# A gated cross-attention and MoE kernel: weight units and first tile re-timed, and half of P's low parts moved to VectorE in the last batch

## What is computed

```
x = x + tanh(g_xattn) * (softmax(q k^T / 8) v) @ Wout      # q from LN(x), k and v from [LN(ctx), LN(x)]
s = softmax(LN(x) @ gate_w); top 2 of 8, renormalised
x = x + tanh(g_ffn) * sum_k s_k * (gelu(LN(x) @ w1[e_k] + b1[e_k]) @ w2[e_k] + b2[e_k])
```

## Time and profile before

| what | us |
|---|---|
| median of 3 runs | 1759.96 (1757.61 to 1762.75) |
| the profiled execution | 1763.63 |
| its span, first to last instruction | 1761.8 |
| TensorE busy | 1652.8 (94%) |
| VectorE, ScalarE, GpSimd busy | 1261.0, 1233.0, 1283.2 |

### The profile page before, as it was taken

The page is one execution under the profiler, slowest core; times in us unless marked ns, Lnnn a source line. Parts: engine busy times, 40 slices in busy tenths (PEclk is TensorE's granted clock), DMA queues, the critical chain, the costliest instruction groups (busy, mean ns, idle before and its releaser), DMA issues.

```text
span 1761.8 us, 42393 instructions
## 1 busy us (share of the span) xinstructions
PE 1652.8 (94%) x14916; PEld 1151.1 (65%) x14916; DVE 1261.0 (72%) x3018; ACT 1233.0 (70%) x2806; POOL 1283.2 (73%) x1448
## 2 busy tenths in 40 slices
PE   3999999999999999999999999999976988899997
PEld 1556666666666666666666666665655777788886
DVE  6777777777877777777777777788865765555553
ACT  3687888878777887877788878877766654444442
POOL 4477888787878888888989879987666554355444
PEclk9999999999999999999999999999988999999999
DMA  4368777777667778767776767755669865444443
GB/s 148 66 128 145 146 146 137 149 149 147 139 136 151 139 140 152 146 138 136 140 146 140 144 132 136 149 107 101 128 136 209 207 134 102 88 73 70 71 68 31
DMA packets 634297, 226.80 MB, mean 129 GB/s; under 512 B 573930, under 2 KB 624914, under 8 KB 633708
## 3 DMA queue, kind: packets, MB, share of 16 engines
q1 hardware_dynamic: 617964, 207.41, 58.6%
q0 software_dynamic: 15552, 16.67, 6.7%
q10 hardware_dynamic: 576, 0.01, 0.0%
HBM read 67.72 MB, written 16.83 MB: 48 GB/s over the span
## 4 chain that ended last, share of the span: by engine, by line
PE 78%; DVE 10%; ACT 4%; issue 3%; POOL 2%; DMA 2%; SPq 0%; POOLq 0%; ACTq 0%; DVEq 0%
PE proj_ps L1446 37%; PE scores_ps L1619 10%; PE scores_ps L1489 9%; PE proj_ps L1632 9%; PE tail_ps L1545 4%; PE pv_ps L1524 4%; PE pv_ps L1526 2%; DVE passed L1090 2%; ACT v_sb L884 2%; DVE v_sb L1245 2%; ACT p_space L804 1%; PE scores_ps L1446 1%; DVE k_lo L1239 1%; POOL p_parts L638 1%; PE proj_ps L1593 1%
## 5 line engine op out<-in xcount | busy, mean ns | idle before, releaser
L638 POOL TENSOR_TENSOR p_parts<-p_space,p_parts 112x487 f16<-112x487 f32 x512 | 560.7, 1118 | 106.4 <-ACT p_parts L813 104.0
L804 ACT ACTIVATE p_space<-scores_ps,shift 112x487 f32<-112x487 f32 x508 | 335.2, 664 | 7.9 <-POOL p_parts L638 5.2
L1090 DVE TENSOR_SCALAR_CACHE_REDUCE passed<-scores_ps 112x487 f16<-112x487 f32 x502 | 302.7, 661 | 24.0 <-PE scores_ps L1489 23.8
L870 ACT ACTIVATE k_hi<-proj_ps 128x488 fp32r<-128x488 f32 x250 | 144.5, 578 | 216.9 <-PE proj_ps L1446 215.3
L813 ACT ACTIVATE p_parts<-p_space 112x487 f16<-112x487 f32 x512 | 276.5, 607 | 0.0
L1245 DVE SCALAR_TENSOR_TENSOR v_sb<-proj_ps,v_sb 128x512 f16<-128x512 f32 x251 | 173.4, 691 | 139.4 <-ACT v_sb L884 128.7
L919 ACT ACTIVATE g_space<-scores_ps,b_sb,undo 128x256 f32<-128x256 f32 x280 | 139.2, 560 | 186.4 <-PE scores_ps L1619 180.9
L1524 PE MATMUL pv_ps<-v_sb,pt_space 128*128 128x128 f16 x2048 | 217.9, 221 | 13.4 <-DMA pt_space<-p_parts 12.0
L1239 DVE TENSOR_TENSOR k_lo<-proj_ps,k_hi 128x488 fp32r<-128x488 f32 x250 | 166.0, 664 | 81.2 <-ACT k_hi L870 79.0
L1619 PE MATMUL scores_ps<-xt_space,arena 128*128 128x256 f16 x1680 | 198.7, 280 | 18.6 <-DVE arena L1135 12.7
L1446 PE MATMUL proj_ps<-kv_hi,wkv_hi 128*128 128x488 f16 x500 | 186.7, 373 | 12.6 <-DVE v_sb L1245 9.3
(11 more groups left out here) (287 smaller groups left out, 3545.9 us busy)
## 6 DMA issues: line engine op xcount, KB each, us to landing
w_part<-in_L_ffn_w_dram SPq DMA_DIRECT2D x64, 256.0 KB, 3.8
arena<-in_L_ffn_w_dram SPq DMA_DIRECT2D x27, 512.0 KB
ctx_sb<-in_ctx_dram SPq DMA_DIRECT2D x32, 375.0 KB
pt_space<-p_parts SPq DMA_TRANSPOSE x256
x_sb<-in_x_dram SPq DMA_DIRECT2D x32, 112.0 KB
res_sb<-in_x_dram SPq DMA_DIRECT2D x32, 112.0 KB
out_dram<-x_sb SPq DMA_DIRECT2D x32, 112.0 KB
xn_dram<-xn SPq DMA_DIRECT2D x32, 112.0 KB
```

The lines of the kernel that those rows point to most:

```text
L638: pool.tensor_tensor(p_parts[0:LQ, p % PS, h, 1, 0:LK], p_f[0:LQ, p % 2, h, 0:LK], p_parts[0:LQ, p % PS, h, 0, 0:LK], ALU.subtract).then_i ...
L804: act.activation(p_f[0:LQ, p % 2, h, 0:LK], score_bank(p, h)[0:LQ, 0:LK], ACT.Exp, bias=shift[0:LQ, p // 2 % 2, n:n + 1], scale=-1.0, accu ...
L1090: dve.tensor_scalar(passed_of(p, h), score_bank(p, h)[0:LQ, 0:LK], P_SHIFT, None, ALU.add, ALU.min, accum_out=shift[0:LQ, p // 2 % 2, n:n ...
```

## The change

The units' tables are rewritten: units 1 to 7 are loaded and units 1 to 3 split earlier, units 15 to 31 are split earlier, and the last loads are spread. Units 1 to 3 get staging room of their own (`EARLY_SLOTS`, in expert 1's region, free once all projections are done). Both turns of rows are at step 251. TensorE makes the first two hidden chunks of tile 0 ahead of step 256. GpSimd writes one entry a step from step 258 on instead of two from step 256 on (two again in the last two steps). `xn16` lies elsewhere, so that unit 19 needs no wait for stores. In the last batch the low part of P for the second head of each pair is made by VectorE, behind the minima of an even step, with a semaphore of its own (`p_low1`) that SyncE and ScalarE wait for besides `p_low`.

```diff
-        if t >= PAIRS:
-            room = 2
+        if t >= PAIRS + 2:
+            room = 1 if t < LAST_STEP - 1 else 2
...
-SPLITS = {-7: (0,), -2: (1,), -1: (2,), 0: (3,), 1: (4,), 2: (5,), 3: (6,), 4: (7,), 7: (8,), 9: (9,), 10: (10,), 11: (11,), 13: (12,), 14: (13,), 15: (14,), 17: (15,),
-          18: (16,), 19: (17,), 21: (18,), 24: (19,), 25: (20,)}
+SPLITS = {-7: (0,), -5: (1,), -4: (2,), -3: (3,), 0: (4,), 1: (5,), 2: (6,), 4: (7,), 6: (8,), 7: (9,), 9: (10,), 10: (11,), 11: (12,), 13: (13,), 14: (14,), 15: (15,),
+          17: (16,), 18: (17,), 19: (18,), 21: (19,), 22: (20,), 23: (21,), 25: (22,)}
 SPLITS = {PAIRS + n: units for n, units in SPLITS.items()}
-TILE_SPLITS = {6: (21,), 7: (22, 23), 8: (24, 25), 9: (26, 27), 10: (28, 29), 11: (30, 31)}
-LOADS = {-16: (0,), -4: (1, 2), -3: (3,), -2: (4,), 0: (5,), 1: (6,), 2: (7,), 4: (8,), 5: (9, 10), 6: (11,), 9: (12,), 11: (13,), 12: (14,), 13: (15,),
-         14: (16,), 15: (17,), 16: (18,), 18: (19,), 19: (20,), 20: (21,), 22: (22,), 26: (23,)}
+TILE_SPLITS = {6: (23, 24), 7: (25, 26), 8: (27, 28), 9: (29, 30), 10: (31,)}
+LOADS = {-16: (0,), -8: (1,), -7: (2,), -6: (3,), -4: (4,), -3: (5,), -2: (6,), -1: (7,), 4: (8, 9), 5: (10, 11), 7: (12,), 8: (13,), 10: (14,), 11: (15,), 12: (16,),
+         14: (17,), 15: (18,), 16: (19,), 18: (20,), 19: (21,), 20: (22,), 22: (23,), 23: (24,), 24: (25,), 26: (26, 28)}
 LOADS = {PAIRS + n: units for n, units in LOADS.items()}
-TILE_LOADS = {6: (24, 28, 29), 7: (25,), 8: (26, 27), 11: (30, 31)}
+TILE_LOADS = {6: (27, 29), 8: (30,), 9: (31,)}
...
-FILL_STEPS = (PAIRS - 5, PAIRS - 3)
+FILL_STEPS = (PAIRS - 5, PAIRS - 5)
...
+        def wait_low(engine, p):
+
+            if p < LAST_PAIR:
+                engine.wait_ge(p_low, 2 * p + 2)
+            else:
+                engine.wait_ge(p_low, LAST_PAIR + p + 1)
+                engine.wait_ge(p_low1, p - LAST_PAIR + 1)
...
                 if u == 1:
+                    sp.wait_ge(proj_done, len(UNITS))
+                if u == 4:
                     sp.wait_ge(pv_done, PAIRS - NP)
...
             def p_low_of(p):
-                for h in range(2):
+                for h in range(2 if p < LAST_PAIR else 1):
...
-                if u == 8:
-                    act.wait_ge(unit_low, 8)
+                if u in (4, 8):
+                    act.wait_ge(unit_low, u)
...
+            def p_low_of(p):
+
+                dve.wait_ge(p_high, 2 * p + 2)
+                dve.tensor_tensor(p_parts[0:LQ, p % PS, 1, 1, 0:LK], p_f[0:LQ, p % 2, 1, 0:LK], p_parts[0:LQ, p % PS, 1, 0, 0:LK], ALU.subtract).then_inc(p_low1, 1)
+
             def unit_low_of(u):
 
-                if u == 19:
-                    for s in range(2):
-                        dve.wait_ge(stored[s], NB // 2 * 32)
...
+                if t % 2 == 0:
+                    for p in (t - 2, t - 1):
+                        if is_pair(p) and p >= LAST_PAIR:
+                            p_low_of(p)
...
             for i in range(-1, TILES):
-                for t in drain(i, 0):
-                    step(t)
+                if i >= 0:
+                    for t in drain(i, 0):
+                        step(t)
...
                     hidden(n, 0, e1)
                     hidden(n, 1, e1)
+                if i < 0:
+                    for t in drain(i, 0):
+                        step(t)
                 for t in drain(i, 1):
                     step(t)
```

More of the change, by code:

```diff
@@ L202, in program @@
             k_lo = at_("k_lo", [128, NP, LKP], F32R)
-            xn16 = at_("xn16", [128, 768], F16)
+            at_("rest4", [128, 384])
             p_parts = at_("p_parts", [128, PS, 2, 2, 512], F16)
@@ L223, in program @@
         sb("rest7", [128, 672])
+        xn16 = sb("xn16", [128, 2 * D], F16)
         experts = arena[:, :].bitcast(F16).rearrange("p (e n) -> p e n", e=E)
@@ L275, in program @@
         quarters = lambda e: [arena[:, (e * REGION // 4) + n * UNIT:(e * REGION // 4) + (n + 1) * UNIT] for n in range(4)]
-        FIRST_SLOTS, STAGE_SLOTS, LATE_SLOTS = quarters(2), quarters(6), quarters(7)
+        EARLY_SLOTS, FIRST_SLOTS, STAGE_SLOTS, LATE_SLOTS = quarters(1), quarters(2), quarters(6), quarters(7)
         SPARE_SLOTS = [wout_hi[:, :, :].rearrange("p j n -> p (j n)").bitcast(F32), wout_lo[:, :, :].rearrange("p j n -> p (j n)").bitcast(F32)]
@@ L306, in program @@
         work = picked[:, :, :, :].rearrange("p a k e -> p (a k e)")
[L307 to L312, removed]
+        slot_space = sb("slot_space", [128, 6, E + 1])
+        slot_expert, slot_row, slot_tiles, slot_used, slot_end, slot_begin = [slot_space[:, n, :] for n in range(6)]
         is_here = sb("is_here", [128, 2, E + 1])
@@ L362, in program @@
         scores_done = sem("scores_done"); shift_done = sem("shift_done"); exp_done = sem("exp_done")
-        p_high = sem("p_high"); p_low = sem("p_low"); p_moved = [sem(f"p_moved{n}") for n in range(PS)]
+        p_high = sem("p_high"); p_low = sem("p_low"); p_low1 = sem("p_low1"); p_moved = [sem(f"p_moved{n}") for n in range(PS)]
         pv_done = sem("pv_done"); inv_done = sem("inv_done"); o_summed = sem("o_summed"); o_scaled = sem("o_scaled"); o_high = sem("o_high"); o_low = sem("o_low")
@@ L459, in unit_staged @@
                 return g_space[:, :]
-            return (FIRST_SLOTS if u < 8 else STAGE_SLOTS if u < 24 else LATE_SLOTS)[u % 4]
+            return (EARLY_SLOTS if u < 4 else FIRST_SLOTS if u < 8 else STAGE_SLOTS if u < 24 else LATE_SLOTS)[u % 4]
         def unit_half(u, a):
@@ L535, in step @@
                     s = p % PS
-                    sp.wait_ge(p_low, 2 * p + 2)
+                    wait_low(sp, p)
                     if p >= PS:
@@ L578, in step @@
                 if t == PAIRS + 2:
-                    sp.wait_ge(p_low, 2 * PAIRS)
+                    wait_low(sp, PAIRS - 1)
                     sp.dma_start(b2_sb, b2.partition_broadcast(128)).then_inc(b2_loaded, 16)
@@ L800, in exponential @@
                 if h == 0 and p >= 2:
-                    act.wait_ge(p_low, 2 * (p - 2) + 2)
+                    wait_low(act, p - 2)
                 n = 2 * (p % 2) + h
```

## The result

The changed kernel took 1746.72 us (median of 5 runs, 1744.35 to 1747.37) against 1759.96 us: ratio 0.9913, 95% interval 0.9894 to 0.9932, so 13 us faster. A second set of 5 runs gave 0.9905 (0.9891 to 0.9919), 1746.88 against 1763.26 us, so 16 us. The forecast was 1741.5 us with a range of 1734 to 1753. The profiled execution took 1746.55 us with a span of 1744.5, 17 us under that of before. That is more than the medians differ by, since the profiled execution of before was 3.7 us above its median.

A forecast was written before the change was run, and what follows sets the result against it. The prediction took TensorE's idle time ahead of 1511.5 us, in waits for VectorE's low halves and in the last attention batch, as what could be won: −14.5 − 4 = −18.5 us from 1760.0 gives 1741.5 us, range 1734 to 1753.

The forecast's parts named there:

- Units 15 to 31 earlier: Tiles 9, 11 and 13: 11.1 us of waits for VectorE's low halves and 3.3 us of slow clock go, 14.5 us.
- A wait for turned rows at tiles 9 to 13: Sign of being wrong: TensorE waiting there for turned rows; no size given.
- Tile 8 waits for gathered rows: Tile 8's rows stand behind four table writes in GpSimd's queue; its wait, 4.12 us before, becomes 4 to 6 us.
- tile 7's 0.98 us: TensorE's wait for a low half at tile 7, counted as no gain since tile 8 waits for rows anyway.
- The low part of the second head on VectorE: Last batch: GpSimd loses 9 us, VectorE pays 8 × 0.66 us, and exponentials wait for subtractions behind four minima.
- The schedule: Last batch: exponentials of pairs 250, 252, 254 at 1308.3, 1317.6, 1327.9 us, all done at 1330.8; tile 1 about 1342.
- The forecast of little contention: Last batch: a VectorE and GpSimd clash costs between nothing and 4.2 us; little was taken.
- Rival C: VectorE shut out at four subtraction steps and three unit splits, 7 × 4.16 = 29 us: 1770 us; chance 0.04.
- The last batch, −4 us in all: Last attention batch: tile 1 at about 1342 us, 3 us early, 4.7 with the clock; −4 us taken.
- Rival B: Last batch: clashes and weight loads bring tile 1 to its old time or up to 7 us later, 1746 to 1755; 0.23.
- A: Rival: VectorE is not in the way, the last batch gives 7 to 10 us: about 1737 us; chance 0.18.
- D: Rival: waits at tiles 9 to 13 only change their name, the last batch gives nothing: 1758 us; chance 0.05.

The follow-up runs named there:

- e2: Kernel before with only the late part of the change, units from 13 on split as in the changed kernel: 1751.7 us, ratio 0.9939.
- e7: Changed kernel with unit 8's load issued one step earlier: 1743.58 us, ratio 0.9891.
- e8: Changed kernel with tile 8's rows fetched by GpSimd ahead of the last four table writes: 1742.48 us, ratio 0.9880.
- e1: Changed kernel with GpSimd making P's low part for both heads in the last batch, as before: 1750.66 us, ratio 0.9925.
- e4: Changed kernel with VectorE's subtraction for pair p - 2 put ahead of the minima of pair p: 1749.19 us, ratio 0.9921.
- e5: Kernel before with one part of the change, VectorE making the second head's low part in the last batch: 1761.41 us, ratio 0.9993.
- e10: Changed kernel with the edits of e1, e7 and e8 together: 1739.42 us, ratio 0.9858.
- e11: e10 with the second table read behind the fetch of tile 9's rows, not in front of it: 1734.44 us, ratio 0.9841.
- e6: Changed kernel with units 12 to 31 loaded and split as in the kernel before: 1760.62 us, ratio 0.9993.

## Why the prediction was right, and where it was off

The time lies in the stated range, and 0.7 us outside the forecast's own 1737 to 1746 us. Against the second set it fits better: a change of 16 us there, 13 in the first, where 18.5 was forecast.

*Units 15 to 31 earlier, −14.5 us: right, 13 us in the traces.* From tile 8 to tile 14 the kernel before needed 1523.67 − 1443.54 = 80.1 us, the changed one 1506.02 − 1438.75 = 67.3, and 66.6 in its second trace: 12.9 and 13.6 us. The terms close to within 0.3 us of the first trace: 11.1 us of waits, 3.3 us of slow clock (before, the granted clock was 0.62 from 1484 to 1488 us and 0.65 from 1511 to 1515), less 0.3 us (tile 8 7.54, not 7.27) and less a new wait of 1.57 us for rows at tile 12. A wait for turned rows at tiles 9 to 13 stood among my signs of being wrong; this one is small, and it did not take the place of the waits that went. Alone (e2) the part gave 13.6 us in the trace and 10.8 in the times.

*Tile 8 waits for gathered rows, 4 to 6 us: right in kind, too small.* 6.3, 8.5 and, in e7, 7.7 us. TensorE comes earlier, and the rows behind the four table writes do not come as much earlier. I had used this only to count tile 7's 0.98 us as nothing; e8 shows that it took some of the early part's gain too.

*The low part of the second head on VectorE: right.* The schedule gave the first exponentials of 250, 252 and 254 at 1308.3, 1317.6 and 1327.9 us; they came at 1305.8, 1315.2 and 1325.7, all 2.2 to 2.5 us earlier, of which 0.85 is the earlier mark and the rest unit 0's split, which I had ending at 1305.4 us. The order behind the minima is worth 2.0 and 1.9 us (e1, e4). The exponentials end 4.3 us later than before, though; in e1, without VectorE's subtractions, they still end 2.3 us later. That is the rest of the early part, in which units 1 to 3 now stand between the exponentials; no run moves these units alone. Subtractions cost 0.62 us each where I had 0.66. The forecast of little contention held: 1.69 us for unit 0. Rival C's subtractions of 2 to 5 us did not occur; the longest pair took 2.17 us. Alone the part is worth nothing (e5).

By the Trainium skill (SBUF — State Buffer, "Who interferes with whom") a VectorE instruction with two SBUF inputs contends with a GpSimd one that reads SBUF, and whichever issues second is blocked for the whole of the other. The rows after fit that: GpSimd's product (L689), 0.61 us as a rule, took 1.61 us beside the 1.69 us split. The 5.44 to 5.46 us of before, e1, e2, e10 and e11, across several GpSimd instructions, are more than that, and e5 shows that GpSimd's second head is the condition.

*The last batch, −4 us in all: the step that was mis-sized.* Tile 1 came at 1341.87 us, as the schedule had it (about 1342), and at full clock; tile 2 is 4.8 us ahead of before. I ended the sum there. The diff also splits unit 8 at step 262, not 263, and its load is issued behind the turn of tile 2's rows: ScalarE waited 6.14 us, and tile 3 was only 1.0 us ahead. At tile 8 3.9 us were left in one execution and 0.4 in the other. Alone the early part is worth 1.2 us in the times, not 4 (e6), and 3.6 in its one trace. Loading unit 8 one step earlier gave 3.3 us (e7), of the 5.2 us by which the forecast missed the median.

*Rival B* (moving work to VectorE gains nothing, 1746 to 1755 us) has the number of the result, 1746.7, and for the moved operation it was right (e1, e5). Its mechanism for the sum, tile 1 at its old time or later, did not happen: tile 1 came at 50.5 us after the mark, not 52.8. That the stated range held is in part luck: what cost most of the difference, unit 8's load queued behind a turn, was in no rival. *A* was wrong (VectorE is in the way), *D* too.

## What to carry to other kernels

When a chain of waits is taken away, carry the schedule on to the next event that is not moved: here a unit split one step earlier than its load allowed, and rows that stood in one engine's queue behind unrelated writes, ate what the front of the stage had won. On in-order queues it pays to put what TensorE waits for first (rows, then table writes, then the table's reading): two such swaps, one earlier load and the low part back on GpSimd (which I could not tell from nothing) were together worth 11 to 13 us by the ratios, nearly as much as the change itself. Where an idle time is named "issue", look at when the data landed.

## What the runs showed of the hardware

- Unit 0's split (those of most other units took 1.28 us) took 5.44 to 5.46 us in every kernel where GpSimd ran 2.17, 0.60 and 2.17 us without a gap, and 1.68 to 1.70 us in every one where it ran one low part, a product and one low part. In the first case VectorE did not get in between two of GpSimd's instructions, in the second it did. Why is not settled.
- From the start of a turn to its last landing it took 3.7 us at tile 8 in the changed kernel (1434.66 to 1438.39) and 7.5 us at tile 4 in e1 (1384.76 to 1392.30). The DMA share was 0.80 and 1.03 in these stretches, but it does not order the turns: tile 8 of the second profile took 4.4 us at 0.93, tile 4 of e7 6.2 us at 0.85. What makes one slow is open.
- The same kernel, profiled twice, differed by 2.9 us at tile 14 (214.6 and 217.5). 0.7 us was there at tile 3, where ScalarE had waited 7.54 us for unit 8's data instead of 6.14; most of the rest came with the rows of tiles 4 and 8. So a difference of 3 us between two single traces of two kernels shows little by itself.
